# Rotary partner rows by two DMAs inside SBUF, in place of a second projection product

## What is computed

```
def _apply_rotary(pos, t):
    half = t.shape[-1] // 2
    rot = jnp.concatenate([-t[..., half:], t[..., :half]], axis=-1)
    return t * jnp.cos(pos) + rot * jnp.sin(pos)

q = split_heads(_proj(x, Wq, bq))     # 8 heads of 16 channels
k = split_heads(_proj(c, Wk, bk))
q = _apply_rotary(q_emb, q)
k = _apply_rotary(k_emb, k)
scores = jnp.einsum('bhtc,bhsc->bhts', q, k) / math.sqrt(K_CH)
```

## Time and profile before

| | |
|---|---|
| median of 3 runs | 3923.88 us (3922.64 to 3927.17) |
| profiled execution | 3921.74 us, of which span 3919.9 us |
| mean granted PE clock over the span | 0.987 |
| busy share of the span | PE 96%, DVE 73%, ACT 60%, POOL 46% |
| cross-attention rounds | from about 842 us to about 1950 us |
| experts after them | to 3919.9 us |

### The profile page before, as it was taken

One profiled execution on the slowest core, in us unless ns is written; L12 is line 12 of the kernel. 1 busy time (PEld: TensorE's weight loads), 2 busy tenths in 40 slices (PEclk: granted clock), 3 DMA queues, 4 the chain that ended last, 5 costly groups with the idle time before them and its releaser, 6 DMA issues.

```text
span 3919.9 us, 74126 instructions
## 1 busy us (share of the span) xinstructions
PE 3775.1 (96%) x24778; PEld 2974.5 (76%) x24778; DVE 2853.0 (73%) x5969; ACT 2340.5 (60%) x5418; POOL 1806.4 (46%) x2121
## 2 busy tenths in 40 slices
PE   7999999979999999999889999999999999999999
PEld 6888888844444444444389999999999999999998
DVE  5777777657888888888746777777777777877333
ACT  5777777647777777776725555555555555555221
POOL 2222223233555555554424556665666665665210
PEclk9999999979999999999999999999999999999999
DMA  5000000023443333444236999999999999998421
GB/s 203 20 26 23 23 23 23 18 79 109 126 124 121 122 123 122 128 133 143 85 102 197 270 260 267 268 267 264 259 268 267 265 267 267 268 267 235 157 94 60
DMA packets 290168, 621.37 MB, mean 159 GB/s; under 512 B 70000, under 2 KB 78576, under 8 KB 289664
## 3 DMA queue, kind: packets, MB, share of 16 engines
q1 hardware_dynamic: 224640, 464.01, 36.3%
q0 software_dynamic: 64000, 150.52, 15.9%
q10 hardware_dynamic: 1152, 2.10, 0.1%
HBM read 459.93 MB, written 155.98 MB: 157 GB/s over the span
## 4 chain that ended last, share of the span: by engine, by line
PE 85%; DVE 7%; ACT 4%; issue 3%; DMA 1%; SPq 1%; POOL 0%; DVEq 0%; ACTq 0%; POOLq 0%
PE ps L525 20%; PE ps L527 18%; PE ps L526 18%; PE ps L701 6%; PE ps L512 4%; PE ps L662 4%; PE ps L684 4%; PE ps L551 3%; PE ps L624 3%; PE ps L795 2%; PE ps L821 2%; ACT PX L973 2%; DVE WD L1454 1%; DVE NM L1306 1%; PE ps L543 1%
## 5 line engine op out<-in xcount | busy, mean ns | idle before, releaser
L525 PE MATMUL ps<-WG,XT 128*128 128x352 f32 x2304 | 765.4, 332 | 8.0 <-DVE XT L1483 5.4
L526 PE MATMUL ps<-WG,XT 128*128 128x352 f32 x2304 | 744.0, 323 | 0.0
L527 PE MATMUL ps<-WG,XT 128*128 128x352 f32 x2304 | 743.9, 323 | 0.0
L973 ACT ACTIVATE PX<-ps 128x1024 f32<-128x1024 f32 x512 | 523.4, 1022 | 261.1 <-PE ps L684 253.7
L1306 DVE TENSOR_REDUCE NM<-ps 128x2 f32<-128x1024 f32 x512 | 622.5, 1218 | 69.3 <-PE ps L662 65.9
L1800 POOL DMA_INDIRECT sum<-YO,TI x224 | 399.2, 1782 | 495.8 <-issue 392.0
L1447 DVE TENSOR_TENSOR WG<-WL,WG 128x704 fp32r<-128x704 f32 x528 | 450.2, 883 | 30.9 <-ACT WG L1086 30.7
L1119 ACT ACTIVATE HS<-ps 128x352 f32<-128x352 f32 x288 | 133.9, 465 | 559.5 <-PE ps L527 559.5
L1489 DVE TENSOR_TENSOR HS<-ps,HS 128x352 f32<-128x352 f32 x288 | 151.0, 524 | 423.6 <-ACT HS L1119 420.1
L525 PEld LDWEIGHTS ps<-WG,XT 128*128 128x128 f32 x2304 | 433.9, 188 | 9.1 <-DVE XT L1483 6.3
L906 ACT ACTIVATE PA<-ps,nb 128x128 f32<-128x128 f32 x1024 | 360.4, 381 | 131.7 <-DVE nb L1175 131.6
(11 more groups left out here) (275 smaller groups left out, 8677.5 us busy)
## 6 DMA issues: line engine op xcount, KB each, us to landing
WL<-in_w_gate SPq DMA_DIRECT2D x128, 704.0 KB, 4.3
WL<-in_w_up SPq DMA_DIRECT2D x128, 704.0 KB, 5.9
DL<-in_w_down SPq DMA_DIRECT2D x128, 512.0 KB, 8.4
kq_parts<-HL SPq DMA_DIRECT2D x64, 512.0 KB, 3.0
KS<-kq_parts SPq DMA_DIRECT2D x384, 64.0 KB
QS<-kq_parts SPq DMA_DIRECT2D x384, 64.0 KB
DL<-in_w_down SPq DMA_DIRECT2D x128, 192.0 KB, 9.1
CB<-sum POOLq DMA_DIRECT2D x64, 256.0 KB, 3.0
```

Source lines behind the costliest of these rows:

```text
L525: pe.matmul(out_, lh(0), rh(0), start=first, stop=False)
L526: pe.matmul(out_, lh(0), rh(1), start=False, stop=False)
L527: return pe.matmul(out_, lh(1), rh(0), start=False, stop=last)
L973: act.activation(PX[:, n % 4, :, :], ps[:, 5 * 512:7 * 512], ACT.Exp, scale=0.25).then_inc(S["a_px"], 1)
```

## The change

PE makes one product per side (rounds 2 and 5) with one weight matrix, and DVE reads its bank twice: first times the sine, then, a round later, times the cosine. The weights' rows are now ordered so that the first halves of all heads lie on partitions 0 to 63 and the second halves on 64 to 127, so the partner of a row is 64 partitions away. A new step `swap` on SP moves the sine product across by two DMAs of 64 partitions within SBUF into TS, a place in XA that the self-attention no longer uses. POOL adds TS in place of T1's second half. Because of the new row order, `away` writes its data by four DMAs in place of one. One of the early weight loads is moved behind the last use of TS.

```diff
-    do(*{..., 2: ("rotate", b + 1, 0, 0), 3: ("rotate", b + 1, 0, 1),
-         4: ("shares", b - 2, 1), 5: ("rotate", b + 1, 1, 0), 6: ("rotate", b + 1, 1, 1), ...
+    do(*{..., 2: ("rotate", b + 1, 0, 1), 3: ("rotate", b + 1, 0, 0),
+         4: ("shares", b - 2, 1), 5: ("rotate", b + 1, 1, 1), 6: ("rotate", b + 1, 1, 0), ...
+    if r == 2:
+        do("swap", b + 1, 0)
+    if r == 5:
+        do("swap", b + 1, 1)
...
-        do("land", piece // 4, piece % 4)
+        do("land", piece // 4, (piece + piece // 4) % 4)
...
+        TS = [XA[:, 4 + kq, :] for kq in range(2)]
...
             def rotate(b, kq, pm):        # PE
+                if pm == 0:
+                    return
...
-                bank0("v_t", 4 * b + 2 * kq + pm + 1)
-                three(bank(0), lambda p: (WXL[:, 2 * kq + pm, :] if p else WXH[:, 2 * kq + pm, :]),
+                bank0("v_t", 4 * b + 2 * kq + 2)
+                three(bank(0), lambda p: (WXL[:, kq, :] if p else WXH[:, kq, :]),
...
             def rotate(b, kq, pm):        # DVE
-                dve.wait_ge(S["p_r"], 4 * b + w + 1)
+                dve.wait_ge(S["p_r"], 2 * b + kq + 1)
...
             def total(b, kq):             # POOL
                 pool.wait_ge(S["v_t"], 4 * b + 2 * kq + 2)
-                pool.tensor_tensor(T1[:, kq, 0, :], T1[:, kq, 0, :], T1[:, kq, 1, :], ALU.add).then_inc(S["l_tt"], 1)
+                pool.wait_ge(S["d_sw%d" % kq], 32 * (b + 1))
+                pool.tensor_tensor(T1[:, kq, 0, :], T1[:, kq, 0, :], TS[kq], ALU.add).then_inc(S["l_tt"], 1)
...
             def away(b, kq):              # SP
-                sp.dma_start(KQ[d, kq, :, :, :].rearrange("r p t -> p r t"), HL[:, d, kq, :, :].bitcast(f32)
-                             ).then_inc(S["d_hl%d" % kq], 16)
+                for h in range(2):
+                    for r in range(2):
+                        sp.dma_start(KQ[d, kq, r, :, :].rearrange("(e h c) t -> h e c t", h=2, c=8)[h],
+                                     HL[64 * h:64 * h + 64, d, kq, r, :].bitcast(f32)).then_inc(S["d_hl%d" % kq], 16)
+
+            def swap(b, kq):
+
+                sp.wait_ge(S["v_t"], 4 * b + 2 * kq + 1)
+                if b:
+                    sp.wait_ge(S["l_tt"], 2 * b + kq - 1)
+                else:
+                    sp.wait_ge(S["d_st%d" % (4 + kq)], 16 * 5)
+                for h in range(2):
+                    sp.dma_start(TS[kq][64 - 64 * h:128 - 64 * h, :], T1[64 * h:64 * h + 64, kq, 1, :]
+                                 ).then_inc(S["d_sw%d" % kq], 16)
```

More of the change, by code:

```diff
@@ L137, in cross_round @@
         do("score", n - LAG)
-    do(*{0: ("keys_of", b, 0), 1: ("maxima", b - 1, 1), 2: ("rotate", b + 1, 0, 0), 3: ("rotate", b + 1, 0, 1),
-         4: ("shares", b - 2, 1), 5: ("rotate", b + 1, 1, 0), 6: ("rotate", b + 1, 1, 1), 7: ("sums", b - 1, 0),
+    do(*{0: ("keys_of", b, 0), 1: ("maxima", b - 1, 1), 2: ("rotate", b + 1, 0, 1), 3: ("rotate", b + 1, 0, 0),
+         4: ("shares", b - 2, 1), 5: ("rotate", b + 1, 1, 1), 6: ("rotate", b + 1, 1, 0), 7: ("sums", b - 1, 0),
          8: ("rank", b - 4), 9: ("maxima", b, 0), 10: ("shares", b - 1, 0), 11: ("turn_g", b - 3), 12: ("keys_of", b, 1),
@@ L397, in build @@
         XB = sb(ax, "XB", [128, NXB, 512])
-        WX, WXL = raw_and_low(ax, "WX", [128, 4, 128])
+        WX, WXL = raw_and_low(ax, "WX", [128, 2, 128])
         WV, WVL = raw_and_low(ax, "WV", [128, 256])
         WO, WOL = raw_and_low(ax, "WO", [128, 2, 128])
-        WXH = sb(ax, "WXH", [128, 4, 128], f32r)
+        WXH = sb(ax, "WXH", [128, 2, 128], f32r)
         WVH = sb(ax, "WVH", [128, 256], f32r)
@@ L1074, in split @@
                 if k == 0:
-                    act.wait_ge(S["p_r"], 4 * NB)
+                    act.wait_ge(S["p_r"], 2 * NB)
                     act.wait_ge(S["p_vx"], 2 * NB)
                 if k < 2:
-                    act.wait_ge(S["d_hl0"], 16 * NB)
-                    act.wait_ge(S["d_hl1"], 16 * NB)
+                    act.wait_ge(S["d_hl0"], 64 * NB)
+                    act.wait_ge(S["d_hl1"], 64 * NB)
                 if k == 1:
@@ L1322, in rotate @@
             def rotate(b, kq, pm):
-                w, tab = 2 * kq + pm, (C_COS, C_SIN)[pm]
-                dve.wait_ge(S["p_r"], 4 * b + w + 1)
-                if b == 0 and w == 0:
+                tab = (C_COS, C_SIN)[pm]
+                dve.wait_ge(S["p_r"], 2 * b + kq + 1)
+                if b == 0 and kq == 0 and pm:
                     dve.wait_ge(S["d_w"], 128 + 16 * NZ)
-                if pm == 0 and b:
+                if pm and b:
                     dve.wait_ge(S["l_lo"], 2 * b + kq - 1)
-                if b == kq == pm == 0:
+                if b == kq == 0 and pm:
                     dve.wait_ge(S["p_s"], 4 * NB)
-                dve.scalar_tensor_tensor(out=T1[:, kq, pm, :], in0=bank(0), scalar=BX[:, w:w + 1],
+                dve.scalar_tensor_tensor(out=T1[:, kq, pm, :], in0=bank(0), scalar=BX[:, kq:kq + 1],
                                          in1=CST[:, tab:tab + 512], op0=ALU.add, op1=ALU.mult).then_inc(S["v_t"], 1)
@@ L1931, in cross_step @@
             def cross_step(name, b, *at):
-                steps = {"gate": gate, "maxima": maxima, "away": away, "stack": stack, "join": join, "norm_g": norm_g,
+                steps = {"gate": gate, "maxima": maxima, "away": away, "stack": stack, "swap": swap, "join": join, "norm_g": norm_g,
                          "load_y": load_y, "load_c": load_c, "land": lambda k, piece: land_shared(k, piece)}
@@ L1959, in land_shared @@
                         sp.wait_ge(S["d_st%d" % i], 16 * XL[i])
+                if k == 1 and piece == 0:
+                    sp.wait_ge(S["l_tt"], 2 * NB)
                 if piece < 2:
@@ L2032, in constants @@
     for r in range(128):
-        d = r % 16
-        c[r, C_COS:C_COS + 512] = cos[:, d % 8]
-        c[r, C_SIN:C_SIN + 512] = -sin[:, d % 8] if d < 8 else sin[:, d % 8]
+        c[r, C_COS:C_COS + 512] = cos[:, r % 8]
+        c[r, C_SIN:C_SIN + 512] = sin[:, r % 8] if r < 64 else -sin[:, r % 8]
     for j in range(4):
@@ L2058, in laid_out @@
     g = {k: np.asarray(v) for k, v in inputs.items()}
-    swap = np.concatenate([np.arange(8, 16), np.arange(0, 8)])
     Wk, Wq = g["L0_xattn_Wk"], g["L0_xattn_Wq"]
-    wx = np.zeros((128, 4, 128), np.float32)
+    wx = np.zeros((128, 2, 128), np.float32)
     bx = np.zeros((128, 7), np.float32)
@@ L2064, in laid_out @@
     wo = np.zeros((128, 2, 128), np.float32)
-    turned = (np.arange(8)[:, None] * 16 + swap[None, :]).ravel()
+    halves = np.arange(128).reshape(8, 2, 8).transpose(1, 0, 2).ravel()
     for kq, (W, b) in enumerate(((Wk, g["L0_xattn_bk"]), (Wq, g["L0_xattn_bq"]))):
-        for pm, r in enumerate((np.arange(128), turned)):
-            wx[:, 2 * kq + pm, :] = W[r, :].T
-            bx[:, 2 * kq + pm] = b[r]
+        wx[:, kq, :] = W[halves, :].T
+        bx[:, kq] = b[halves]
     for hh in range(2):
```

12 lines of the change are left out of this document (6 added, 6 removed).

## The result

The changed kernel takes 4020.3 us (median of 4 runs, 4004.15 to 4030.8) against 3925.21 us (median of 4 runs, 3922.64 to 3927.17) for the kernel before: ratio 1.0237, 95% interval 1.0209 to 1.0266. It is some 95 us slower. The forecast was 3920, and the range of 3900 to 3942 doesn't hold the time. The profiled execution took 4014.51 us, span 4012.7, mean granted clock 0.963 against 0.987.

What follows compares the result with a forecast made beforehand. DVE, not PE, was taken to bound rounds 1 to 6, where the removed products stand. Gains of 6 and 1.1 us less 3.3 lost made 3.8 us faster, 3920 us, with a range of 3900 to 3942.

Steps and rivals of the forecast that it cites:

- The bound, and the gain of PE's part: Cross-attention: DVE bounds rounds 1 to 6, so removing 1.8 us of PE gains 0.2 us per sequence, 6 us in all.
- rival A: PE is the bound after all: 30 x 1.8 = 54 us gained, about 3867 us; chance 7%.
- The ramp: Where the self-attention runs out, one product shortens a chain of waits: 1.1 us gained once, bounds 0 and 3.
- The swap hidden: Partner rows of round 5's swap land by 1429.6 to 1430.3, POOL needs them at 1430.30: cost 0.
- the four writes: SP's queue, rounds 11 to 1: three more issues of 0.43 add 1.3 us; 3.3 us lost in all, bounds 0 and 8.
- fits both: Growth of 1.3 us fits the slack ahead of round 4's `score` (2.2 us) and round 0's `top` (2.0 us).
- The forecast's 2.2 us: Slack of SP's chain: 0.3 us ahead of maxima plus 1.9 until the `score` of round 4 must start.
- Where SP was late already: Sequences where SP was last, or weight loads precede maxima: 1.2 us lost at the worst, 1.3 more per full wait.
- rival B: SP's chain is late; `top` of round 0 and `score` of round 4 wait some 0.5 us each: 3940 to 3949; 18%.
- Rival C: Holes in rounds 3 and 6 let PE's clock fall once per sequence: 90 us lost, about 4010; chance 5%.

Runs made afterwards that it cites:

- x9: The changed kernel with its 128 rows ordered by channel, then head, so one write replaces the four; swaps unchanged: 3929.22 us, ratio 1.0009.
- x4: The changed kernel with one write and no swaps (POOL adds the unexchanged sine half): 3929.48 us, ratio 1.0006.
- x3: The changed kernel with the one write of before, both swaps kept, so heads read their neighbours' rows: 3929.72 us, ratio 1.0002.
- x10: The kernel x9, but PE makes each rotary product twice again, one write and both swaps kept: 3928.18 us, ratio 1.0001.
- x1: The kernel before with all four products and no swap, but rows in halves and four 8x8x512 writes as in the changed kernel: 3976.29 us, ratio 1.0121.
- x2: The kernel before in its own row order, with each write as four plain DMAs of 64x512: 3953.88 us, ratio 1.0059.
- x5: The changed kernel, swaps and four writes included, but PE makes each product a second time: 3980.0 us, ratio 1.0126.
- x14: The kernel x9 with both value products moved behind the top of rounds 3 and 6, reads together, ACT copying ox and HL first: 4007.78 us, ratio 1.0203.

## Why the prediction was wrong

**The bound, and the gain of PE's part.** Right in kind: removing 1.8 us of matmul from a sequence gave 0.13 to 0.14 us (x9, x4), where 0.2 was forecast, and rival A (54 us) is refuted. The forecast said that the 0.2 would come from round 7. The hole in front of its `score` is there, 0.88 us; that the gain comes from it was not shown.

**The ramp** (1.1 us) is below what the times can tell. The traces are in line with it: from the first maxima to 937 us x9, x4 and x3 gain 1.7 to 2.1 us on the kernel before, and the bounds were 0 and 3.

**The swap hidden.** Right: x3, x10.

**The failed step: the four writes, priced at 3.3 us in all ("Three more issues add 3 x 0.43 = 1.3 us", "Growth of 1.3 fits both").** x1 measures them at 48 us. Three things were wrong in it.

*The growth* is 2.3 us (5.14 less 2.84), 2.6 by the medians. The issue was mis-sized: 0.43 was the stack's row, while a piece of 64 partitions takes 0.59, so away's issues take 2.51 us in place of 0.38, 2.1 more. And no piece landed sooner: from the end of the last issue to the stack it is 2.63 us (1418.06 less 1412.92 and 2.51), and 2.46 before. The chain of x2 has grown by 1.64 us at the stack and 1.55 to the end of stack(1,1) (medians, 14.53 against 12.98), near what the forecast had.

*Where growth costs.* The table compares the same evictions NT of ACT in the profiled executions: how many us later each comes than in the kernel before, whose own stand at 937, 1760 and 1934 us.

| kernel | at 937 | at 1760 | at 1934 |
|---|---|---|---|
| x2, four plain writes | 7.9 | 8.5 | 28.0 |
| x1, four writes | 8.6 | 28.9 | 47.9 |
| x5, four writes and swaps, PE full | 13.8 | 41.7 | 59.9 |
| the changed kernel | 13.2 | 57.1 | 86.4 |
| x9, one write, one product | -2.0 | 2.8 | 3.6 |
| x10, one write, PE full | 6.4 | 6.4 | 6.3 |

The growth of x2 costs 0.6 us over the 24 sequences from 937 to 1760: for it "fits both" held. The growth of x1 costs 20 there, though PE is as full. Its chain has grown by 2.40 us to the end of stack(1,1), so the slack of a usual sequence lies somewhere between 1.55 and 2.40. The forecast's 2.2 us came from one sequence with a good start: there stack(1,1) ended 1417.53 - 1405.14 = 12.39 us after away(1), in the median of 23 sequences at 12.98, at worst at 13.54.

*Where SP was late already*, the forecast put some 3 us, with each wait 1.3 longer. From 1760 us on, with the weight loads in the queue, every kernel with four writes loses 18 to 29 us, x2 among them (19.5). Waits of up to 3.6 us and the half clock behind them make it up; the forecast priced neither the further waits nor the clock there. The first column is not the writes' alone, since x10, with one write, is 6.4 us late there.

This is rival B, priced too low as well: 3940 to 3949, where x1 measures 3976. B had no cost for the clock, and summed over windows of 10 us x1 stands at half clock for 51 us and x2 for 38, where the kernel before has 8. That is up to 21 and 15 us of their loss, with PE full.

The Trainium skill (DMA: Bandwidth & Descriptors, "Why a DMA increments its semaphore by 16 and not by 1") was set beside that step: by its rule the 8x8x512 writes use 8 engines, and growth would be 1.6. The pair x1 and x2 agrees with the rule's direction: the same bytes and number of issues, but from the last issue to the stack 2.59 us with 8x8x512 and 2.02 with plain rows (medians 2.83 and 1.97), and 22 us more in the time. No row counts the engines.

**Rival C, at 5%, is in the other half, but not as it was told.** Alone, the holes bring one fall in the steady rhythm (x9, x4, x3), not one for each sequence; that C's 4010 is near the measured time is chance. C was set aside because the clock stood at 1.00 with PE busy 3.99 of 6.00 us. That one window is at the end of the stretch and says only that a single gap may pass. The pair x5 and the changed kernel shows 40 us that go when PE is kept full; x9 shows the fall behind two waits in rounds 4 and 5. The forecast weighed B and C apart. They add up. How is in part argued: SP's late data would lengthen the holes that the product leaves, the clock falls, and the slower matmuls hold all others up. The Trainium skill (TensorE: Matmul & The Clock Gate, "A second HAM failure mode: psum-queue depth-cycling") describes falls from short idles between groups of matmuls; the traces of x14 and the changed kernel agree (0.91 and 0.93 in the windows above), while x9 with its holes fell once (0.69) and then had 1.00 over 750 us.

The four corners, by medians: one write with PE full 3925 (before) and 3928 (x10), one write with one product 3929 (x9), four writes with PE full 3976 (x1) and 3980 (x5), four writes with one product 4020. Four writes cost some 50 us, the missing product 1 to 4 alone and 40 beside them.

What stays open: why equal holes bring the clock down in some sequences and not in others, and how the 40 us divide between the clock and longer waits for the maxima (42.6 against 23.0 us); and what makes x5 and x10 late before 937 us.

## What to carry to other kernels

Price a split DMA by its issue on the queue that is tight and by the landing of its new shape, from rows of that shape if there are any, and take the slack from the median and the worst of all sequences, not from one. Then look apart at the stretches in which the queue has other work: a chain that is hidden in every steady sequence (x2) still cost 20 us where weight loads stood in it. Look first for a layout in which the partner is far but the rows still leave in one write. Taking matmuls off an engine that waits for another gave nothing here and opened holes; where data also came late, much more was lost than the matmuls had cost, and the granted clock was down. Before relieving a queue by issuing from another engine, see what stands behind the issue there.

## What the runs showed of the hardware that was not expected

- The issue of a write of 64 partitions by 512 elements took 0.59 us on SP in either form, more than that of the whole 128x2x512 (0.38).
- In x9 two waits of PE of 0.97 and 0.43 us, with PE about 90% busy in the 20 us that end with them, were followed by a fall to half clock; over the 750 us from 1030 on the same kernel ran at a mean of 1.00.
- In mid-stretch x14's clock fell in every sequence of 37.55 us, with a mean of 0.91.
- In x2, with PE full, a single wait of 2.51 us at 1773 us was followed by matmuls of 0.79 in place of 0.40, and the clock over 1760 to 1960 us was 0.91.
- Two DMA issues on ACT held it for 1.17 us, and the next instruction came 1.30 us after the eviction's.
